# Perceiver block on one core: the scores of a head cut at 512, 1024, 1408 and 1792 in place of 512, 1024, 1536 and 2048

## The reference, cut to what matters

```python
kv_len = q_len + context.shape[1]                      # 128 + 2048 = 2176
scores = jnp.einsum('bqhgd,bkhd->bhgqk', q, k) * scale
attn = jax.nn.softmax(scores.astype(jnp.float32), axis=-1).astype(q.dtype)
out = jnp.einsum('bhgqk,bkhd->bqhgd', attn, v)
out = out.reshape(b, q_len, N_HEADS * HEAD_DIM)
return out @ Wo
```

## Time and profile before

| | |
|---|---|
| three runs | 662.74, 660.14 and 662.64 us, median 662.64 us |
| span of the profiled execution | 660.8 us |
| TensorE busy | 97% of the span |
| VectorE, ScalarE, GpSimd busy | 68%, 55%, 31% |
| mean granted clock of TensorE | 0.997 |

### The profile page before, as it was taken

How to read it: one execution, slowest core, us unless ns; L and a number is a source line. 1 busy time by engine, 2 the same in 40 slices (tenths; PEclk the granted TensorE clock), 3 DMA queues, 4 the chain that set the end, 5 groups by cost and what they waited for, 6 DMA issues and landing times.

```text
span 660.8 us, 12479 instructions
## 1 busy us (share of the span) xinstructions
PE 640.7 (97%) x4212; PEld 547.9 (83%) x4212; DVE 450.6 (68%) x1056; ACT 362.6 (55%) x711; POOL 202.9 (31%) x150
## 2 busy tenths in 40 slices
PE   7999999999999999999999989998999999999998
PEld 6788888898899989998999869987788797797473
DVE  3533143788787878887887655978976856758873
ACT  3413125777787778777867834766344545446210
POOL 0000000644674478446844544002320220200000
PEclk9999999999999999999999999998999999999999
DMA  7711002236253443526242746673667668687600
GB/s 257 268 63 64 1 0 73 75 75 192 67 175 98 147 123 87 183 72 193 59 130 68 260 190 168 242 298 104 243 214 287 229 220 287 219 340 296 256 1 16
DMA packets 27224, 104.80 MB, mean 159 GB/s; under 512 B 7424, under 2 KB 7808, under 8 KB 17584
## 3 DMA queue, kind: packets, MB, share of 16 engines
q1 hardware_dynamic: 26608, 103.23, 46.4%
q10 hardware_dynamic: 576, 1.05, 0.6%
HBM read 86.30 MB, written 0.26 MB: 131 GB/s over the span
## 4 chain that ended last, share of the span: by engine, by line
PE 84%; DVE 4%; POOL 4%; ACT 3%; DMA 2%; issue 2%; SPq 0%; ACTq 0%; DVEq 0%
PE ps L1451 19%; PE ps L1222 14%; PE ps L1223 13%; PE ps L1224 13%; PE ps L1491 8%; PE ps L1342 4%; PE ps L1299 3%; POOL pt_lo L428 3%; PE ps L1480 2%; DMA ring<-wv_dram 2%; PE ps L1601 2%; PE ps L1564 1%; DVE acc L1053 1%; PE ps L1471 1%; POOL k_lo L428 1%
## 5 line engine op out<-in xcount | busy, mean ns | idle before, releaser
L1451 PEld LDWEIGHTS ps<-norm_t,ring 128*128 128x128 f32 x1152 | 132.0, 192 | 4.9 <-issue 4.1
L1451 PE MATMUL ps<-norm_t,ring 128*128 128x128 f32 x1152 | 133.4, 276 | 0.0
L1053 DVE SCALAR_TENSOR_TENSOR acc<-raw,cw,acc 128x127 f32<-128x127 f32 (+2 forms) x240 | 85.0, 429 | 24.7 <-ACT acc L707 24.0
L428 POOL TENSOR_TENSOR pt_lo<-far_t,pt_hi 128x512 fp32r<-128x512 f32 (+1 forms) x75 | 87.3, 1183 | 37.7 <-ACT pt_hi L521 37.4
L1222 PE MATMUL ps<-pt_hi,v_hi 128*128 128x256 f32 x272 | 84.6, 311 | 3.0 <-POOL pt_lo L428 2.7
L521 ACT ACTIVATE pt_hi<-ps 128x512 fp32r<-128x512 f32 (+1 forms) x69 | 41.0, 595 | 68.1 <-PE ps L1342 68.1
L1224 PE MATMUL ps<-pt_lo,v_hi 128*128 128x256 f32 x272 | 76.6, 282 | 0.0
L1223 PE MATMUL ps<-pt_hi,v_lo 128*128 128x256 f32 x272 | 76.5, 281 | 0.0
L912 DVE TENSOR_SCALAR_CACHE_REDUCE prob_near<-ps 128x512 f32<-128x512 f32 x64 | 44.2, 691 | 24.5 <-PE ps L1224 22.7
L814 DVE TENSOR_TENSOR pt_lo<-ps,pt_hi 128x512 fp32r<-128x512 f32 (+1 forms) x69 | 47.3, 687 | 19.0 <-ACT pt_hi L521 17.5
L428 POOL TENSOR_TENSOR wo_lo<-ring,wo_hi 128x1024 fp32r<-128x1024 f32 x16 | 38.5, 2407 | 70.7 <-ACT wo_hi L521 70.7
(11 more groups left out here) (197 smaller groups left out, 1311.2 us busy)
## 6 DMA issues: line engine op xcount, KB each, us to landing
ring<-w_in_dram SPq DMA_DIRECT2D x36, 1024.0 KB, 4.9
far_t<-blocks_t SPq DMA_DIRECT2D x240, 72.0 KB, 2.0
ring<-w_out_dram SPq DMA_DIRECT2D x16, 1024.0 KB, 4.8
ring<-wq_dram SPq DMA_DIRECT2D x8, 1024.0 KB, 5.1
ring<-wo_dram SPq DMA_DIRECT2D x8, 1024.0 KB, 7.1
w_sb<-w_dram SPq DMA_DIRECT2D x4, 896.0 KB, 9.1
ring<-ctx_t_dram SPq DMA_DIRECT2D x3, 1024.0 KB, 7.2
ring<-w_dram SPq DMA_DIRECT2D x3, 1024.0 KB, 9.1
```

The source lines that it names most:

```text
L428: sub = lambda dst, a, hi: pool.tensor_tensor(dst, a, hi, ALU.subtract)
L1053: ins = nc.vector.scalar_tensor_tensor(a[:, i, back:], r[:, i, 0:T - back], cw[:, bass.ds(tile + i, 1), 3 - back:4 - back].rearrange("p a ...
L1451: ins = mm(ps[:, bank, t * T:t * T + T], w[:, t, c, :], norm_t[:, c, :], start=(c == 0), stop=(c == NC - 1))
```

## The change

The borders of the pieces are given by a table. The pieces of a head have 512, 512, 384, 384 and 384 keys. Their number, banks, places in the units and semaphores stay. The same `chunk_cols` cuts the splitting of the keys, so `k_hi` and `k_lo` get the new pieces as well.

```diff
 NCHUNK = 5
+EDGES = (0, 512, 1024, 1408, 1792, 2176)
@@
 def chunk_cols(c):
 
-    return c * BANK, min((c + 1) * BANK, KV_LEN)
+    return EDGES[c], EDGES[c + 1]
```

## The result

The changed kernel takes **658.06 us** (median of four runs, 657.4 to 660.73 us) against 662.25 us for the kernel before in the same comparison (four runs, 660.14 to 662.74 us). The ratio is 0.9945, its 95% interval 0.9926 to 0.9965. The forecast was 657.9 us. Two runs of the kernel before that belong to later comparisons, of 805 and 2654 us, were slow ones and enter no ratio.

A forecast was written before the change was run, and what follows sets the result against it. TensorE, busy 97% of the 660.8 us span, was taken as the bound. Cheaper triples 4.3, less 0.7 lost in waits, plus 1.1 for the third wait, save 4.7 us: 662.64 to 657.9 us, eight-in-ten range 655.0 to 661.6 us.

The forecast's parts named there:

- the price of a triple (A): TensorE's score triples: with 384 columns 0.525 us each, a head falls from 3.09 to 2.955 us; 32 heads save 4.3 us.
- The half that waits absorb (B): Steps 0, 2, 6, 10 and 14: TensorE's first-half saving only lengthens waits for GpSimd, 5 x 0.135 = 0.7 us lost.
- The third wait (C): TensorE's wait before piece 3 ahead in steps 2, 6 and 10 goes: 0.38 us each, 1.1 us in all.
- the 0.15 us of room: Steps 2, 6 and 10: `k_lo` of piece 3 done at 239.69, 0.15 us before TensorE wants it at 239.84.
- What costs nothing: VectorE's score work keeps its sum, head 0's `neg_max` stays in time, and far-block transfers land in time: no cost.
- Head 0's room: Time between head 0's maximum being done and ScalarE asking for it: 0.62 us before, 0.48 us left after.
- The far moves: Far-block transfers land at 227.9, ScalarE needs them at 228.81; the 0.9 us shrink by 0.27 us.
- Saved time handed back: Rival: TensorE's saving returns as waits for GpSimd in all fifteen steps and the third wait stays: 660.3 us, chance 0.17.
- Columns alone: Rival: TensorE's triples cost only by columns, so only the third wait's 1.1 us is won: 661.5 us, chance 0.12.
- A dear 384 triple: Rival: 384-column triples cost more than the line; at 0.69 us the kernel takes 673.7 us; chance 0.06.
- The late maximum: Rival: head 0's `neg_max` comes late, delaying ScalarE, GpSimd and TensorE; 660 to 665 us, chance 0.03.

The follow-up runs named there:

- experiment 2: Scores cut in the changed kernel's pieces, keys split in the old pieces of the kernel before: 658.79 us, ratio 0.9946.
- experiment 10: Experiment 9's kernel, with GpSimd doing `k_lo` of pieces 2 and 3 ahead of `pt_lo(8)`: 657.71 us, ratio 0.9937 against the kernel before.
- experiment 1: Pieces of 512, 512, 128, 512 and 512 keys, compared with the kernel before: 661.2 us, ratio 0.9994.
- experiment 3: Changed kernel with pieces of 512, 512, 512, 384 and 256 keys: 657.89 us, ratio 0.9939 against the kernel before.
- experiment 4: Changed kernel with pieces of 512, 512, 512, 448 and 192 keys: 659.19 us, ratio 0.9958 against the kernel before.
- experiment 8: Changed kernel with `k_lo` of piece 0 of each new key head on VectorE, between its two far transposes in unit 2: 656.54 us, one run.
- experiment 9: Experiment 8's kernel, with ScalarE making `pt_hi(6)` ahead of `k_hi` of piece 1: 656.21 us, ratio 0.9917 against the kernel before.
- experiment 6: Changed kernel with `k_lo` of piece 0 of each new key head on VectorE in unit 4, not GpSimd: 658.1 us, ratio 0.9937.

## Why the prediction held, and where it was off

**The bound and the price of a triple (A).** Forecast 0.135 us a head, 4.3 us in all. A plain step fell by 0.24 to 0.25 us where two heads made 0.27; over 16 pairs 3.9 us. The 384 triple was taken at 0.525 us and has 0.52 to 0.53. The half step of head 1 gave 0.14 us as forecast, that of head 0 0.11: the sum was made of distances read to 0.01 us, and a hundredth on a triple is 1 us over 96.

**The half that waits absorb (B).** Forecast 5 x 0.135 = 0.7 us. In steps 2, 6, 10 and 14 the waits grew by 0.11 to 0.13 us, as the mechanism has it. In step 0 the wait shrank from 0.67 to 0.54 us, so nothing was lost there: 4 x 0.12 = 0.5 us. Why step 0 differs no run shows.

**The third wait (C).** Forecast 0.38 us three times; such a step was to fall by 0.27 - 0.135 + 0.38 = 0.515 us, and steps 2, 6 and 10 fell by 0.49 to 0.54 us. The wait was for `k_lo` of piece 3 (experiments 2 and 10), and the 0.15 us of room counted for it were enough. The working has A and C side by side, and experiment 2 shows that they are one: without C those three steps keep 18.60 us.

**The sum.** 3.9 - 0.5 + 1.1 = 4.5 us against 4.6 us measured in the stretch and 4.7 us forecast; A was taken 0.4 us too large and B 0.2 us, which offset each other in part. The span was to be 656.1 us and is 654.7 us; the difference is no part of the change. That the median, 658.06 us, lies within 0.2 us of the forecast is luck: the changed kernel's later medians were 656.14 and 656.91 us. What held is the gain in the stretch.

**What costs nothing.** Right in what it cost: ScalarE waits for `neg_max` once, at the start of the attention, as before the change. Head 0's room went from 0.62 to 0.54 us where 0.48 us were reckoned, and a piece of 384 columns takes VectorE 552 ns where the line gave 554. The far moves were in time. But the working looked at head 0 alone, and head 1 is the one without room: 0.03 us before and 0.04 us after in step 5. Nothing in the working showed that head 1's maximum would be in time; that it was is luck so far as the working goes. With 512 columns last it was late (experiment 1).

**The rivals.** Saved time handed back: no new wait in eleven plain steps, and the third wait gone. Columns alone: refuted by the plain steps and by experiments 3 and 4. The rule behind it, in the Trainium skill, TensorE: Matmul & The Clock Gate, section Back-to-back issue gap, gives 56 ns for 128 columns and 216 ns for 512, as the gap of an isolated matmul. The same section says that this counts too little for small matmuls in a stream with weight loads, and has 81 ns and 131 ns there; the prediction left that out. The triples show 110 ns and 230 ns a matmul, so neither pair holds here. A dear 384 triple: 0.52 us. The late maximum: it costs the changed kernel nothing; with 512 columns last ScalarE is late by 0.20 us a plain step, and TensorE still doesn't wait for it.

## What to carry to other kernels

When each matmul brings a weight load of its own, cut the work so that no piece falls under the number of columns where its price stops falling (here about 256); how the rest is divided hardly matters, as 512, 384 and 256 at the end or three of 384 show. Where an engine is paced by another's chain, price the whole step by that chain: a saving on the waiting engine is worth nothing there alone, and a wait taken away comes back at the next operation that hangs on the same chain (experiments 8 to 10 took 1.25 us of work off GpSimd's chain and got at most 0.17 us of a step). Compare the stretch that a change touches, not the span, when other stretches vary by more than the change.

## What the runs showed that I had not expected

**The clock fell at one idle time or at another.** Behind the attention TensorE has idle times of 2.0 us (for `o_lo`) and 2.6 us (for `yv`) that no cut of the scores touches. After the second, the granted clock before the change, windows of 2 us (length, TensorE busy, granted clock, share and rate of the transfers):

```profile
454.00:456.00 2.00, 2.00 (x8) 0.50 0.30 119
456.00:458.00 2.00, 2.00 (x17) 0.83 0.00 0
```

And after the change, behind the first of them and behind the second:

```profile
386.00:388.00 2.00, 2.00 (x9) 0.50 0.87 340
```

```profile
448.00:450.00 2.00, 1.65 (x12) 1.00 0.96 401
450.00:452.00 2.00, 2.00 (x19) 1.00 0.00 0
```

0.50 is the level of 1.2 GHz. Before, the group of the state-space layer behind the 2.6 us (from its `xc` transposes to those of the next group) took 27.61 us and after the change 26.01 us; the stretch behind the attention (from the last `values` to the first group's `xc` transposes) took 39.17 us before and 39.98 us after. Together 0.8 us of the span's 6.1 us. It is not the kernel that decides: the changed kernel profiled again had 39.16 and 26.01 us, with neither fall, and a third time 39.98 and 26.01 us. Of thirteen profiles, all kernels of this study together, five show the 27.6 us and seven the 40.0 or 40.2 us, one of them both. What decides whether the clock falls at an idle time was not tried.

**What VectorE and GpSimd pay side by side.** VectorE took 1.82 and 1.41 us for a subtraction of 0.69 us (experiments 6 and 8); in both the excess is the rest of a GpSimd instruction already under way, less about 0.1 us. In experiment 8 that is the second of two `pt_lo` that begin at 227.15 us and last 2.52 us together, to 229.67 us; VectorE ends 0.55 us after it. GpSimd in turn took 0.41 us longer for the two `pt_lo` that followed in experiment 6.
